# A graph attention kernel: the edge scores summed on VectorE, the one-hots of the look-ups and all weightings on ScalarE

## What is computed

```python
xl = (x @ Wl + bl).reshape(n, h, d)
xr = (x @ Wr + br).reshape(n, h, d)
e = leaky_relu(xl[src] + xr[dst], 0.2)
score = einsum('ehd,hd->eh', e, att)
m = segment_max(score, dst)
ex = exp(score - m[dst])
alpha = ex / segment_sum(ex, dst)[dst]
out = segment_sum(alpha[:, :, None] * xl[src], dst)
```

## Time and profile before

| what | value |
|---|---|
| median of 3 runs | 6380.7 us (6372.31 to 6382.09) |
| profiled execution | 6354.12 us |
| its span | 6352.2 us |
| mean granted TensorE clock | 0.922 |
| busy over the span | DVE 86%, PE 78%, ACT 72%, POOL 60%, PEld 46% |

### The profile page before, as it was taken

How to read it: one execution, slowest core, us unless ns; L and a number is a source line. 1 busy time by engine, 2 the same in 40 slices (tenths; PEclk the granted TensorE clock), 3 DMA queues, 4 the chain that set the end, 5 groups by cost and what they waited for, 6 DMA issues and landing times. The chain is left out here.

```text
span 6352.2 us, 127992 instructions
## 1 busy us (share of the span) xinstructions
PE 4973.3 (78%) x23046; PEld 2906.5 (46%) x23047; DVE 5465.1 (86%) x13020; ACT 4594.8 (72%) x19630; POOL 3833.8 (60%) x3546
## 2 busy tenths in 40 slices
PE   3797799935888999998878898988889766656663
PEld 2574355512444444444463444444444455555553
DVE  9989988843999999999966999999999866666666
ACT  5576799921999999999926999999999653333332
POOL 0588777784666666666503666666666217777773
PEclk9999999967999999999989999999999977777775
DMA  0262000023555555555604555555555334444444
GB/s 13 58 79 33 2 2 2 2 45 86 147 137 140 139 139 139 139 139 140 123 17 144 139 140 139 140 139 140 141 140 139 67 95 128 130 127 129 127 129 78
DMA packets 352738, 655.93 MB, mean 103 GB/s; under 512 B 110151, under 2 KB 201221, under 8 KB 352116
## 3 DMA queue, kind: packets, MB, share of 16 engines
q0 software_dynamic: 185888, 481.62, 30.1%
q1 hardware_dynamic: 166612, 172.14, 11.0%
HBM read 617.73 MB, written 33.88 MB: 103 GB/s over the span
## 5 line engine op out<-in xcount | busy, mean ns | idle before, releaser
L1268 POOL DMA_INDIRECT feat_area<-xl_table,feat_area x1856 | 1992.5, 1074 | 1499.2 <-PE bank L1342 679.4
L1419 ACT ACTIVATE feat_area<-feat_area 128x130 f32<-128x130 f32 x5568 | 1643.5, 297 | 185.1 <-DVE feat_area L1472 182.6
L1329 PE MATMUL bank<-node_area,feat_area 128*128 x3712 | 1464.8, 518 | 339.6 <-DVE feat_area L1464 176.2
L1403 ACT ACTIVATE feat_area<-feat_area 128x128 f32<-128x128 f32 x4640 | 1442.2, 387 | 31.6 <-issue 31.6
L1342 PE MATMUL bank<-feat_area 128*128 128x390 f32 x3712 | 1405.3, 501 | 34.3 <-ACT feat_area L1403 8.4
L634 POOL DMA_INDIRECT rec_by_dst<-feat_area,gather_col x800 | 979.0, 1224 | 243.7 <-issue 235.5
L1906 POOL DMA_INDIRECT feat_area<-kv_table,gather_src x832 | 808.8, 972 | 467.0 <-issue 252.3
L1329 PEld LDWEIGHTS bank<-node_area,feat_area 128*128 128x128 f32 x3712 | 631.8, 190 | 986.9 <-issue 727.7
L1419 ACT ACTIVATION_READ_ACCUMULATOR feat_area<-feat_area 128x1 f32 x5568 | 1040.3, 187 | 0.0
L1342 PEld LDWEIGHTS bank<-feat_area 128*128 128x128 f32 x3712 | 668.5, 190 | 602.2 <-issue 192.9
L1464 DVE TENSOR_TENSOR feat_area<-bank,feat_area 128x780 f32<-128x780 f32 x928 | 885.9, 955 | 22.3 <-DMA feat_area<-xl_table,feat_area 14.9
(11 more groups left out here) (336 smaller groups left out, 6999.9 us busy)
## 6 DMA issues: line engine op xcount, KB each, us to landing
feat_area<-lo_slot SPq DMA_DIRECT2D x464, 128.0 KB, 3.3
feat_area<-xl_table,feat_area POOLq DMA_INDIRECT x1856, 3.4
feat_area<-lo_slot_src SPq DMA_DIRECT2D x104, 256.0 KB, 3.5
node_area<-lo_edge SPq DMA_DIRECT2D x100, 256.0 KB
xl_table<-feat_area SPq DMA_DIRECT2D x98, 195.0 KB, 2.3
feat_area<-kv_table,gather_src POOLq DMA_INDIRECT x832, 2.8
rec_by_dst<-feat_area,gather_col POOLq DMA_INDIRECT x800
feat_area<-gates SPq DMA_DIRECT2D x348, 32.0 KB
```

The lines of the kernel that those rows point to most:

```text
L1268: pool.indirect_dma_start(ring[:, at:at + HE], None, k.xl, bass.IndirectOffsetOnAxis(ap=index[s // CG][:, n:n + 1], axis=0)).then_inc(gath ...
L1329: last = nc.tensor.matmul(pair[s % 2][:, u, 0:HE], pick[s // 2 % 2][:, c:c + P], k.node[:, ds(columns[0], HE)], start=True, stop=True)
L1403: last = nc.scalar.activation(row[:, 0:D], row[:, 0:D], ACT.Copy, scale=row[:, D:D + 1])
L1419: last = nc.scalar.activation(at, at, ACT.Copy, accum_out=score[s // CG][:, to:to + 1])
```

## The change

VectorE's product `weigh` becomes six instructions a group, one per tile and head, of 130 columns each, which give their running sum as the score (`accum_out`). ScalarE's `reduce` is gone. ScalarE makes the look-ups' one-hots instead, in two passes, |partition - lane| into `away` and then relu(1 - away), and weighs all heads of all groups. The z buffers go from four to two, and `first_lane` has lead 3 in place of 4.

```diff
-    V = 4
+    V = 2
...
+    away = cut(2 * GS * P)
...
             def sums(j, s):
...
-                pe.wait_ge(byvec, CG * j + s // 2 + 1)
...
             def turn(j, s):
...
-                pe.wait_ge(reduced, U * j + s + 1)
+                pe.wait_ge(weighed, U * j + s + 1)
...
         def _(act):
...
             def weight(j, s):
                 act.wait_ge(weights, chunk(j, s) + 1)
                 for u in range(GS):
-                    for h in range(H - 1 if s % 2 == 0 else H):
+                    for h in range(H):
...
-            def reduce(j, s):
...
+            def picks(j, s):
+                if s % 2:
+                    return
                 g = U * j + s
...
+                act.wait_ge(lo_ready[s // 2 % 2], 16 * (4 * j + s // 4) + 16)
+                if later(g, 2):
+                    act.wait_ge(picked, CG * j + s // 2)
+                nc.scalar.activation(away, lo_bc[s // 2 % 2], ACT.Abs, scale=-1.0, bias=k.part_f[:, 0:1]).then_inc(away_set, 1)
+                act.wait_ge(away_set, CG * j + s // 2 + 1)
+                if later(g, 4):
+                    act.wait_ge(looked, g - 2)
+                if s % CG == 4:
+                    act.wait_ge(lane_set, chunk(j, s) + 1)
+                nc.scalar.activation(pick[s // 2 % 2], away, ACT.Relu, scale=-1.0, bias=k.ones[:, 0:1]).then_inc(picked, 1)
...
-            pipeline(act, groups, [(-3, exps), (-11, weight), (0, reduce)], U)
+            pipeline(act, groups, [(-3, exps), (-11, weight), (4, picks)], U)
...
         def _(dve):
...
-            def picks(j, s):
...
             def add(j, s):
...
-                    dve.wait_ge(reduced, g - V + 1)
+                    dve.wait_ge(weighed, g - V + 1)
...
             def weigh(j, s):
                 g = U * j + s
                 dve.wait_ge(added, g + 1)
-                zu = z[s % V].rearrange("p (u e) -> p u e", u=GS)
-                nc.vector.scalar_tensor_tensor(out=zu, in0=zu, scalar=0.0, in1=att_w.unsqueeze(1).to_broadcast([P, GS, HE]),
-                                               op0=ALU.max, op1=ALU.mult).then_inc(weighed, 1)
+                c = chunk(j, s)
+                if s % CG == 0 and later(c, 2):
+                    dve.wait_ge(turned, c - 1)
+                for u in range(GS):
+                    for h in range(H):
+                        at = z[s % V][:, u * HE + h * DW:u * HE + (h + 1) * DW]
+                        to = h * CROW + s % CG * GS + u
+                        last = nc.vector.scalar_tensor_tensor(out=at, in0=at, scalar=0.0, in1=att_w[:, h * DW:(h + 1) * DW],
+                                                              op0=ALU.max, op1=ALU.mult,
+                                                              accum_out=score[s // CG][:, to:to + 1])
+                last.then_inc(weighed, 1)
...
-            def weight(j, s):
...
-                                   (-2, carry), (0, weigh), (-2, spread_fwd), (-3, spread_weights), (-11, weight),
-                                   (4, picks), (-2, spread_bwd), (4, first_lane)], U)
+                                   (-2, carry), (0, weigh), (-2, spread_fwd), (-3, spread_weights), 
+                                   (-2, spread_bwd), (3, first_lane)], U)
```

More of the change, by code:

```diff
@@ L1243, in gat_edges @@
     index_set, lo_ready, gate_set = ([k.sem(f"a{tag}_{n}{s}") for s in range(2)] for n in ("index", "lo", "gate"))
-    names = ("loaded", "order", "preset", "picked", "looked", "added", "weighed", "reduced", "placed", "weighted",
-             "byvec", "summed", "acced", "fixed")
-    (loaded, order, preset, picked, looked, added, weighed, reduced, placed, weighted, byvec, summed, acced,
+    away = cut(2 * GS * P)
+    names = ("loaded", "order", "preset", "picked", "looked", "added", "weighed", "away", "placed", "weighted",
+             "summed", "acced", "fixed")
+    (loaded, order, preset, picked, looked, added, weighed, away_set, placed, weighted, summed, acced,
      fixed) = (k.sem(f"a{tag}_{n}") for n in names)
```

## The result

The changed kernel takes 6613.4 us (median of 4, 6609.5 to 6615.9) against 6381.4 us: a ratio of 1.0365, with a 95% interval of 1.0352 to 1.0378. It is **3.65% slower, 232 us**. That lies in the range given (6335 to 6730) and on the side that was given the most weight, but the likeliest forecast was +15 us.

A forecast was written before the change was run, and what follows sets the result against it. VectorE was taken to bound the edge stages: per chunk +2.70 us for cut products, -3.05 for moved work, +0.48 for reads, +0.13 x 116 = +15 us, so 6396 us against a median of 6380.7; range 6335 to 6730.

The forecast's parts named there:

- the likeliest forecast: Whole kernel: +15 us, 6396 us against a median of 6380.7; chance 0.43 for 6360 to 6475.
- VectorE bounds, priced by its steps: Edge stages: VectorE, busy 495 of 500 us, is the limit, so costs are its start-to-start times.
- chunk: Unit of the edge-stage sums: eight groups, 27.4 us; 116 in both stages, so 0.1 us each is worth 11.6 us.
- The read of the accumulator: VectorE, after each product piece: a second instruction, 48 a chunk, whose added step was taken as 10 ns.
- r: The step on VectorE that one accumulator read adds; break-even at 7 ns, chosen as 10 ns.
- The read costs a small operation: Rival, VectorE's reads: each steps 68 ns like a copy of 3 columns, +338 us, 6719 us; chance 0.25.
- The summing form at half rate: Rival, VectorE's products: summing halves throughput, 754 us on top, 7150 us; chance 0.06.
- ScalarE has room, its picks aren't late: ScalarE, edge stages: 20.9 us of a chunk's 27.4, picks with 7 us slack; rival of late picks, 7077 us, chance 0.04.
- The one-hots at 1.71 us a chunk: VectorE: the four look-up one-hots that move to ScalarE free 1.71 us a chunk.
- The sum of these: VectorE, per chunk: 2.70 for the pieces, less 3.05 for moved work, plus 0.48 for reads, +0.13 us.
- Each product becomes six of 130 columns: VectorE's products: six steps of 0.203 us, 1.22 against 0.88 us a group, +2.70 us a chunk.
- If VectorE isn't at 99% in the edge stages [...] my reading of who bounds is wrong: Sign for the profile after: VectorE below 99% busy in the edge stages would refute VectorE as the limit.

The follow-up runs named there:

- e3: The changed kernel with the running sums left out (`accum_out` dropped, scores zero), so no accumulator reads; ratio 0.9915 against the kernel before.
- e8: The changed kernel with VectorE's list of the edge stages written out straight, without a loop; ratio 0.9983 against the kernel before.
- e10: The changed kernel with VectorE's list straight and VectorE making the look-ups' one-hots again, ScalarE only weighing; ratio 1.0327 against the kernel before.
- e9: The kernel before with VectorE's list of the edge stages written out straight, without a loop; ratio 0.9995 against the kernel before.
- e5: The kernel before with nine increments of two spare semaphores behind VectorE's addition in each group, 382 records a turn; ratio 1.0366.

## Why the prediction was right and wrong

- **VectorE bounds, priced by its steps:** right. Six products step 0.203 us each (e3). Without sums a chunk was to be 0.35 us shorter: in e3's timeline it takes a median 27.10 us, where the kernel before has 27.46, so 0.36. The total, at 0.9915, gives 54 us / 116 = 0.47, a little more.
- **The read of the accumulator:** right. r was chosen as 10 ns; it is 10 to 12. It shows as 11 or 12 ns more before the read and 0 after it. From chunk to chunk, e8 (27.57) against e3 (27.10), it is 10 ns a sum. "The read costs a small operation" (68 ns) would have given +338 us and is refuted by the same steps; the total came to lie between it and my forecast for another reason. ScalarE's read, a full small step, was no guide to VectorE's.
- **The summing form at half rate,** from the Trainium skill ("Vector Engine (DVE) Microarchitecture Reference", points that are easy to get wrong): refuted for this form. A product of 130 columns takes 286 ns with a sum and 284 without, both inputs fp32 in SBUF.
- **ScalarE has room, its picks aren't late:** right. 332 of 500 us busy, and 356 in e8; VectorE waits for it once in each stage, 4.6 and 4.3 us.
- **The one-hots at 1.71 us a chunk:** a little low, 1.9 (e10).
- **The sum of these,** +0.13 us a chunk: e8 against e9 has +0.10. In all, e8 stands 0.1% under e9 where the chunks say 0.2% over it. The two intervals overlap, and VectorE's wait for gathered rows fell from 17.5 us in e9 to 10.7 in e8; the rest of that difference stays open.
- **The step that failed is one that the sum didn't have.** "Each product becomes six of 130 columns" was counted as engine time alone, not as instructions: with the reads, and less what left VectorE, 150 records more in each turn of a loop. The chain went: list of 388 records, fetch at every branch, VectorE idle for 3.5 us, 52 times, 182 us of the trace's 257. Another 0.5 us a chunk, 58 us over 116 chunks, is the later issue that goes with the loop, and 12 us are the +0.10 of the operations. That leaves 5 us; VectorE's wait for TensorE at L1544 is 9 us longer than before (14.1 against 5.0 at the former L1555), the one at L1500 isn't. The forecast's own test, "If VectorE isn't at 99% in the edge stages [...] my reading of who bounds is wrong", pointed there: 463 of 500. The trace of the kernel before had a sign of it that the forecast didn't read: ScalarE's 26 "issue" waits at L1403 in the second stage.
- The range held the time because it took in a dear read, which didn't happen and whose price of +338 us is more than what did happen. As to the cause that is luck.

## What to carry to other kernels

When an edit splits an instruction, count the list of one loop turn as well as engine time: a body that outgrows what is kept pays a fetch at every branch, here 3.5 us, and it shows as idle time of kind "issue" at the first operation of a turn. Look for such rows on every engine of the kernel before: on one that doesn't bound they cost nothing, and they are a warning that lists of this size may be fetched again. The cure is fewer turns (a longer body, or a straight list) or fewer instructions, and it needs no change to the work. A sum on VectorE's product is nearly free; what it costs is the cut into pieces, 0.34 us for one into six.

## What was unexpected of the hardware

- A loop body of VectorE of 292 or 322 records (sequencer included) shows no gap, 382 and 388 show one of some 3.5 to 4.7 us at each branch, 366 shows it in one stage and not in the other, and so does ScalarE's of 301. So the length in records alone doesn't decide. Straight code, of which there was a whole stage in e8, shows no such gap.
- On VectorE the accumulator's read takes 77 ns in the records but moves nothing: the following operation starts at the same time. On ScalarE its step is 0.09 us.
- Nine increments of semaphores a group, small work of the sequencer behind an operation of 0.88 us, cost the kernel 3.7%, 230 us, and VectorE's two rows in e5 come to 212 (of which the kernel before has 15.6 too).
